# Expert biases as the weight of a constant last element, and scatters ahead of the reciprocal root, in an attention and mixture-of-experts kernel

## The chip, the cores and the metric

The kernel runs on one core of a Trainium2 chip. The metric is the device time of one execution in microseconds. Five engines work side by side: TensorE (PE in the profile, with its weight loads as PEld), VectorE (DVE), ScalarE (ACT), GpSimd (POOL) and SyncE (SP, which here only issues transfers). Sixteen DMA engines carry the transfers.

## What is computed

The reference takes x (64 sequences of 128 tokens, 256 features) and a context (64 x 128 x 192) and does, in float32:

```python
x = x + cross_attention(layernorm(x), ctx)      # 16 heads of 64, per sequence; Wproj, bproj
x = x + ffn(layernorm(x))
# ffn: probs = softmax(tokens @ gate_w.T)        # 8 experts
#      top2_w, top2_idx = top_k(probs, 2)
#      expert_out = silu(tokens @ expert_w[e].T + expert_b[e])
#      mixed = sum over the two chosen experts of top2_w * expert_out
#      out = mixed @ combine_w.T
```

The layernorm has no scale and no shift, so the 256 elements of a normalised row sum to zero (but for rounding).

## The kernel before

**Pairs and slots.** The 8192 tokens are 32 pairs of 256 tokens. The program of each engine is one loop over slots s, written `slots()`, with i = s // 8 the pair and u = s % 8 the position in it; slots -8 to -1 are the start. A slot handles two of the sixteen heads of pair i as a pipeline over several slots: queries and keys (`qk_ps`), scores (`s_ps`), the exponential on ACT (L828, into `probs`, which lies in `stage`), the sums on DVE (L1015), the division on POOL (`normalise_probs`, L1309), the transposes on PE (`pT_ps`, L607, the first PE work of a slot), attention times values (`o_ps`), its split into a high and a low part on POOL (`split_attended`, L1318 and L1320), and the projection (`proj_ps`). Float32 products are made of three matmuls of float32r parts: hi x hi, hi x lo, lo x hi; ACT makes the high parts and DVE or POOL the low ones.

**Norms.** DVE makes the statistics (bn_stats, bn_aggr), POOL the reciprocal root (`rsqrt`, L1299 to L1304: an add of eps and a pow), DVE the normalised rows (`normalise`, L992). For the second norm (n = 1) of pair i - 1 all three steps stand in slots u = 2 and u = 3 of pair i.

**Experts.** 28 pairs (SPARSE) go the sparse way. After the routing of a pair, POOL scatters its normalised rows `xn2` by expert into `sorted_x` with four indirect DMAs, one in each of the slots u = 0 to 3 two pairs later (`scatter`, L1322). When a chunk of pairs (8, 8, 6, 4, 2) is routed, DVE lists its blocks of 128 rows of one expert (`list_blocks`), 147 in all, and from then on one block a slot is loaded, transposed (`turn_block`), multiplied with the expert's weights (`expert`, L693), put through silu as tanh, and stored in `sorted_y`. POOL gathers the results (`gather`), ACT weighs them, PE transposes their sum and multiplies it by the combine weights (`combine`); such a pair of steps is a mix. The last 4 pairs go the dense way after attention is over: `dense` (L715) makes all experts' outputs for 256 tokens in 8 jobs a pair, each with a 512 wide result, and `dense_out` and `dense_add` on DVE collect them.

**Biases.** The expert biases are split into high and low parts and stored in a small table (`keep_bias`, L435). Each block loads its expert's two rows (`b_block`, L474), and a seventh matmul of ones with that tile adds them. Each dense job has a seventh matmul too, of `first_two` (ones in two rows) with `b_all` (L722 to L726).

**First loads and splits.** SP issues the loads of x, context and weights in the order of L497 to L508. The expert weights (256 x 2048) come in two halves of 128 rows, `WEIGHTS[6]` and `[7]`, over parts of `stage` that earlier weights held, so SP waits for DVE's splits first (L422). In slots 0 to 7 ACT makes the high part of one expert's weights (`weight_hi`, L804), POOL the low part (`weight_lo`, L1288), and SP stores both in `expert_table` (`keep_expert`, L428). Transfers issued by SP stand in one queue, the keys' spread `k_s<-qk_s` (L412) among them, without which no scores start.

Of the kernel before, what the change touches and what calls it, by code (L numbers as in the profile page):

```python
# [18 lines left out]
ROUND = 8388608.0  # L19

# [116 lines left out]
def xattn_moe_kernel(nc, x, ctxT, wq, wkv, wkv_rest, wproj, bproj, gateT, expertT, expert_b, combineT, out):  # L137
# [19 lines left out]
    bias_table = nc.dram_tensor("bias_table", [(REGIONS + 1) * 2, C], F32, kind="Internal").ap()  # L157

    with ExitStack() as stack:
# [15 lines left out]
        gate_raw = sb("gate_raw", [P, 2, E])  # L175
        pbias = sb("pbias", [P, C], F32R)
# [3 lines left out]
        first_two = sb("first_two", [P, P], F32R)  # L180
# [20 lines left out]

        bias_raw = xn2[1][0:E + 1, 0, :]
        bias_s = [xn2[0][0:E + 1, h, :].bitcast(F32R) for h in range(2)]
# [4 lines left out]
        b_block = [sb(f"b_block{r}", [P, C], F32R) for r in range(RING)]  # L208
        xbT = [hilo(f"xbT{b}", [P, 2, P]) for b in range(2)]
        mT_s = hilo("mT_s", [P, 2, N2])  # L210

# [30 lines left out]
        b_all = wkvr_s[0]  # L242
# [57 lines left out]
        bias_stored = sem("bias_stored")  # L300
# [8 lines left out]
        b_block_in = [sem(f"b_block_in{r}") for r in range(RING)]  # L309
# [33 lines left out]
        two_zero = sem("two_zero")  # L343
# [13 lines left out]
        def blocks_in_ring(r, n):  # L357
# [11 lines left out]
            (expertT[P:2 * P, :], stage[:, 1, :]),  # L369
# [22 lines left out]
        def _(sp):  # L392
# [42 lines left out]
            def keep_bias():  # L435
                sp.wait_ge(ebias_lo, 1)
                of_expert = bias_table.rearrange("(e h) c -> e h c", h=2)
                for h in range(2):
                    of = bias_s[h].bitcast(F32)
                    sp.dma_start(of_expert[0:E, h, :], of[0:E, :]).then_inc(bias_stored, 16)  # L440
                    sp.dma_start(of_expert[E:E + 1, h, :], of[0:1, :]).then_inc(bias_stored, 16)
                    sp.dma_start(of_expert[E + 1:E + 2, h, :], of[E:E + 1, :]).then_inc(bias_stored, 16)
                sp.wait_ge(bias_stored, 96)
                sp.wait_ge(zeroed, 2)
                sp.dma_start(pbias[0:2, :].bitcast(F32), bias_table[2 * (E + 1):2 * (E + 2), :]).then_inc(bias_in, 16)
# [14 lines left out]
            def load_expert(c, b, n):  # L460
# [7 lines left out]
                if n == 0:  # L468
                    sp.wait_ge(bias_stored, 96)
# [4 lines left out]
                sp.dma_start(b_block[r][0:2, :].bitcast(F32),  # L474
                             bias_table[bass.ds(e * 2, 2), :]).then_inc(b_block_in[r], 16)
# [17 lines left out]
            def load_biases():  # L493
                sp.dma_start(b_all[0:2, :].bitcast(F32).rearrange("h (e c) -> h e c", e=E),
                             bias_table[0:2 * E, :].rearrange("(e h) c -> h e c", h=2)).then_inc(dense_in[0], 16)

# [66 lines left out]
        def _(pe):  # L563
# [56 lines left out]
            def project(j, p):  # L620
# [5 lines left out]
                if j == 0 and p == HEAD_PAIRS - 1:  # L626
                    pe.wait_ge(bias_in, 16)
                    pe.wait_ge(const_r, 3)
# [40 lines left out]
            def gate(j, bank):  # L669
                pe.wait_ge(drained["turn_x1"], j + 1)  # L670
                if j == 0:
                    pe.wait_ge(gate_w_ready, 2)
# [5 lines left out]
            def rank(j, bank):  # L678
                pe.wait_ge(hot_done, j + 1)
                if j == 0:  # L680
                    pe.wait_ge(const_r, 3)
# [11 lines left out]
            def expert(n, bank):  # L693
                pe.wait_ge(drained["turn_block"], n + 1)
                pe.wait_ge(w_block_in[n % RING], 16 * (n // RING + 1))
                pe.wait_ge(b_block_in[n % RING], 16 * (n // RING + 1))
# [4 lines left out]
                terms.append((ones_s[:, :], b_block[n % RING][:, :]))  # L701
# [13 lines left out]
            def dense(n):  # L715
                m, q, t = SPARSE + n // DENSE_JOBS, n % DENSE_JOBS // 2, n % 2
                if n == 0:
                    pe.wait_ge(dense_in[0], 80)
# [711 lines left out]
```

## Time and profile before

| | us |
|---|---|
| median of 3 runs (lowest, highest) | 1630.62 (1629.04, 1634.59) |
| the profiled execution, its own time | 1637.44 |
| its span, first to last instruction | 1635.4 |
| busy in it: PE, DVE, ACT, POOL | 1537.0, 1264.0, 1062.0, 879.9 |

The durations below are of the profiled execution, whose time is 0.4% above the median of the others. A matmul's printed duration runs from its start to a modelled end and overlaps the next one; starts of neighbours show the pace. In the timeline view a row is: start, duration, engine, line, operation, out<-in, shape, and in brackets the idle time before it with what ended it.

### The profile page before, as it was taken

How to read it: one execution, taken by the hardware profiler on the slowest of the kernel's cores; microseconds unless marked ns; L12 is line 12 of the kernel's file. 1: busy time of each engine (PE TensorE's matmuls, PEld its weight loads, DVE VectorE, ACT ScalarE, POOL GpSimd, SP SyncE). 2: the span in 40 equal slices, each digit the busy share in tenths (PEclk: the TensorE clock that was granted, in tenths of full speed). 3: DMA queues.
4: the chain of work that ended last, by engine and by line, in shares of the span. 5: the costliest groups of instructions: out<-in, count | busy, mean ns of one | idle time of the engine just before them, and what ended most of it. 6: DMA issues, size and time to landing. Idle time of an engine off the chain costs nothing.

```text
span 1635.4 us, 39352 instructions
## 1 busy us (share of the span) xinstructions
PE 1537.0 (94%) x11891; PEld 1470.2 (90%) x11891; DVE 1264.0 (77%) x3135; ACT 1062.0 (65%) x2890; POOL 879.9 (54%) x1185
## 2 busy tenths in 40 slices
PE   4999999998999999999999999999999999999787
PEld 4899999998999999998999999899998998999675
DVE  5788888777888888877877888877778787776566
ACT  4766666665666766675767667666766666666433
POOL 4655555555545555576655545575656465644410
PEclk9999999999999999999999999999999999999999
DMA  6633333333577777344677667467777776877722
GB/s 226 203 85 91 92 91 92 91 91 95 173 216 223 223 217 210 101 123 128 201 224 227 204 213 217 135 188 226 230 227 211 220 229 198 248 218 216 273 64 78
DMA packets 179131, 286.99 MB, mean 175 GB/s; under 512 B 23575, under 2 KB 113900, under 8 KB 178668
## 3 DMA queue, kind: packets, MB, share of 16 engines
q1 hardware_dynamic: 168172, 255.11, 52.7%
q0 software_dynamic: 10752, 29.37, 5.8%
q8 instruction: 99, 1.62, 0.4%
q14 instruction: 108, 0.88, 0.2%
HBM read 155.66 MB, written 61.62 MB: 133 GB/s over the span
## 4 chain that ended last, share of the span: by engine, by line
PE 73%; DVE 10%; issue 6%; ACT 5%; POOL 4%; DMA 1%; SPq 0%; ACTq 0%; DVEq 0%; POOLq 0%
PE gen_ps L566 21%; PE qk_ps L566 15%; PE o_ps L566 9%; PE proj_ps L566 9%; PE s_ps L566 8%; PE pT_ps L607 6%; ACT stage L801 2%; PE gen_ps L690 1%; PE gen_ps L657 1%; PE gen_ps L665 1%; DMA k_s<-qk_s 1%; DVE sums L1015 1%; ACT v_s_hi L801 1%; POOL sorted_x L1328 1%; POOL stage L1309 1%
## 5 line engine op out<-in xcount | busy, mean ns | idle before, releaser
L828 ACT ACTIVATE stage<-s_ps,neg_max 128x128 f32<-128x128 f32 x1024 | 292.8, 371 | 105.8 <-DVE neg_max L1008 95.7
L1318 POOL CAST o_s_hi<-stage 128x256 fp32r<-128x256 f32 x256 | 102.2, 399 | 477.0 <-ACT stage L801 471.8
L1309 POOL TENSOR_TENSOR stage<-stage,inv_sums 128x512 f32<-128x512 f32 x256 | 266.8, 1042 | 15.9 <-DVE inv_sums L1017 15.9
L801 ACT CAST pT_s_hi<-pT_ps 128x512 fp32r<-128x512 f32 x256 | 150.9, 589 | 150.9 <-PE pT_ps L607 141.8
L566 PE MATMUL s_ps<-k_s,qk_s 128*128 128x256 f32 x1536 | 226.6, 283 | 4.1 <-DMA k_s<-qk_s 3.2
L1015 DVE TENSOR_REDUCE sums<-stage 128x4 f32<-128x512 f32 x256 | 172.9, 676 | 66.5 <-ACT stage L828 56.7
L960 DVE TENSOR_TENSOR pT_s_lo<-pT_ps,pT_s_hi 128x512 fp32r<-128x512 f32 x256 | 172.8, 675 | 56.0 <-ACT pT_s_hi L801 50.3
L960 DVE TENSOR_TENSOR qk_s<-qk_ps,qk_s 128x512 fp32r<-128x512 f32 x256 | 175.8, 687 | 41.8 <-ACT qk_s L801 39.0
L566 PEld LDWEIGHTS s_ps<-k_s,qk_s 128*128 128x128 f32 x1536 | 201.4, 191 | 4.9 <-DMA k_s<-qk_s 3.9
L1320 POOL TENSOR_TENSOR o_s_lo<-stage,o_s_hi 128x256 fp32r<-128x256 f32 x256 | 188.0, 734 | 21.1
L801 ACT CAST v_s_hi<-gen_ps 128x512 fp32r<-128x512 f32 x129 | 75.7, 587 | 177.2 <-PE gen_ps L566 173.3
L801 ACT COPY stage<-o_ps 64x256 f32<-64x256 f32 x512 | 188.4, 368 | 3.1
L566 PE MATMUL qk_ps<-xT_hi,wq_s_hi 128*128 128x256 f32 x512 | 166.7, 326 | 11.4 <-DVE wkvr_s_lo L971 6.5
L566 PE MATMUL o_ps<-pT_s_hi,v_s_hi 128*128 128x256 f32 x512 | 156.0, 305 | 22.4 <-DVE pT_s_lo L960 19.2
L1008 DVE TENSOR_REDUCE neg_max<-s_ps 128x4 f32<-128x512 f32 x256 | 174.4, 681 | 2.5 <-PE s_ps L566 2.5
L801 ACT CAST qk_s<-qk_ps 128x512 fp32r<-128x512 f32 x256 | 152.8, 597 | 24.8 <-PE qk_ps L566 18.2
L566 PE MATMUL proj_ps<-wproj_s_hi,o_s_hi 128*128 128x256 f32 x512 | 149.5, 292 | 12.5 <-POOL o_s_lo L1320 12.5
L607 PE MATMUL pT_ps<-ident,stage 128*128 128x128 f32 x1024 | 156.9, 276 | 2.2 <-POOL stage L1309 1.0
L566 PE MATMUL o_ps<-pT_s_lo,v_s_hi 128*128 128x256 f32 x512 | 145.2, 284 | 0.0
L566 PE MATMUL o_ps<-pT_s_hi,v_s_lo 128*128 128x256 f32 x512 | 145.2, 284 | 0.0
L566 PE MATMUL qk_ps<-xT_lo,wq_s_hi 128*128 128x256 f32 x512 | 144.5, 282 | 0.0
L566 PE MATMUL proj_ps<-wproj_s_hi,o_s_lo 128*128 128x256 f32 x512 | 143.9, 281 | 0.0
(358 smaller groups left out, 4706.1 us busy)
## 6 DMA issues: line engine op xcount, KB each, us to landing
w_block<-expert_table SPq DMA_DIRECT2D x147, 512.0 KB
k_s<-qk_s SPq DMA_DIRECT2D x512, 128.0 KB
stage<-sorted_x SPq DMA_DIRECT2D x147, 128.0 KB
sorted_y<-stage SPq DMA_DIRECT2D x147, 128.0 KB
x_raw<-in_x SPq DMA_DIRECT2D x32, 256.0 KB
c_raw<-in_ctxT SPq DMA_DIRECT2D x32, 256.0 KB, 3.3
stage<-in_x SPq DMA_DIRECT2D x32, 256.0 KB
x_kept<-x SPq DMA_DIRECT2D x32, 256.0 KB
```

The costliest lines, as they stand in the source:

```text
L566: mm = pe.matmul(out_ap, l, r, start=start and n == 0, stop=stop and n == len(terms) - 1, skip_group_check=skip)
L607: mm = pe.transpose(pT_ps[:, k * P:(k + 1) * P], probs[p % 2][:, k, :], ident[:, :])
L657: mm = pe.matmul(bank[:, a * N2 + t * P:a * N2 + (t + 1) * P], src[:, 2 * t + k, a * P:(a + 1) * P], ident[:, :], is_transpose=True, start ...
L665: mm = pe.transpose(bank[:, a * N2 + t * P:a * N2 + (t + 1) * P], src[:, t, a * P:(a + 1) * P], ident[:, :])
L801: last = act.copy(to, of)
L828: last = act.activation(probs[p % 2][:, k, :], s_ps[:, k * P:(k + 1) * P], ACT.Exp, bias=neg_max[p % 2][:, k:k + 1])
L960: last = dve.tensor_tensor(lo, of, hi.bitcast(F32), ALU.subtract)
L1008: dve.tensor_reduce(neg_max[p % 2][:, :], s_ps[:, :].rearrange("p (k n) -> p k n", k=4), AX_X, ALU.max, negate=True).then_inc(max_done, 1)
L1015: dve.tensor_reduce(sums[p % 2][:, :], probs[p % 2][:, :, :], AX_X, ALU.add).then_inc(sums_done, 1)
L1309: pool.tensor_tensor(probs[b][:, :, :], probs[b][:, :, :], inv_sums[b][:, :].unsqueeze(2).broadcast_to([P, 4, P]), ALU.mult).then_inc(prob ...
L1318: pool.tensor_copy(hi[:, :, :], o_full).then_inc(o_hi, 1)
L1320: pool.tensor_tensor(lo[:, :, :], o_full, hi[:, :, :].bitcast(F32), ALU.subtract).then_inc(o_lo, 1)
```

## The change

The last element of each row of the second norm is not computed: it is 1.0 always (set once in both `xn2` buffers; `normalise` writes 255 elements). Since a normalised row sums to zero, the product with a weight matrix is the sum over the other 255 elements with the last element's weights subtracted from theirs. So the last weight row becomes free to hold the bias. DVE subtracts the last row, which SP loads into all partitions for each expert (`load_last`), from the expert's weights (`expert_minus_last`); the second half of the expert weights is loaded without its last row, whose place takes `expert_b`. The same is done for the gate weights, with no bias (there the last row becomes zero). The bias matmuls of blocks and of dense jobs, their loads and their table go. `bproj` keeps its way, with its two parts now copied straight to `pbias`. On POOL, the four scatters of a pair stand ahead of `rsqrt` in their slot.

```diff
             (expertT[0:P, :], stage[:, 0, :]),
-            (expertT[P:2 * P, :], stage[:, 1, :]),
+            (expertT[P:2 * P - 1, :], stage[0:P - 1, 1, :]),
...
             def keep_bias():
                 sp.wait_ge(ebias_lo, 1)
-                of_expert = bias_table.rearrange("(e h) c -> e h c", h=2)
+                sp.wait_ge(zeroed, 2)
                 for h in range(2):
-                    of = bias_s[h].bitcast(F32)
-                    sp.dma_start(of_expert[0:E, h, :], of[0:E, :]).then_inc(bias_stored, 16)
...
+                    sp.dma_start(pbias[h:h + 1, :].bitcast(F32), bias_s[h].bitcast(F32)).then_inc(bias_in, 16)
+
+            def load_last(e):
+
+                wait(sp, minus_last, 2 * (e - RING + 1))
+                sp.dma_start(last_row[:, e % RING, :], expertT[2 * P - 1:2 * P, e * C:(e + 1) * C].broadcast_to([P, C])).then_inc(
+                    last_in[e % RING], 16)
...
                 sp.dma_start(w_block[r][:, :, :].bitcast(F32).rearrange("p a n -> p (a n)"),
                              expert_table[bass.ds(e * P, P), :]).then_inc(w_block_in[r], 16)
-                sp.dma_start(b_block[r][0:2, :].bitcast(F32),
-                             bias_table[bass.ds(e * 2, 2), :]).then_inc(b_block_in[r], 16)
...
-            sp.dma_start(bias_raw[0:E, :], expert_b.rearrange("(e c) -> e c", c=C)).then_inc(ebias_in, 16)
-            sp.dma_start(bias_raw[E:E + 1, :], bproj.rearrange("(e c) -> e c", c=C)).then_inc(ebias_in, 16)
+            sp.dma_start(gate_last[:, :], gateT[C - 1:C, :].broadcast_to([P, E])).then_inc(gate_in, 16)
+            sp.dma_start(bias_raw, bproj.rearrange("(e c) -> e c", c=C)).then_inc(ebias_in, 16)
             for n in range(5, 9):
                 load_weights(n)
+                if n == 7:
+                    sp.dma_start(stage[P - 1:P, 1, :], expert_b.rearrange("(o n) -> o n", o=1)).then_inc(w_in[7], 16)
+                    for e in range(RING):
+                        load_last(e)
...
+                if 0 <= s < E - RING:
+                    load_last(s + RING)
...
                 if s == SLOTS * pairs - 3:
                     load_experts(0)
-                    load_biases()
...
                 for a in range(2):
                     terms += three(xs, (w[:, a, :], w[:, 2 + a, :]), lambda y: y[:, a, :], lambda part: part)
-                terms.append((ones_s[:, :], b_block[n % RING][:, :]))
                 return products(bank[:, 0:C], terms)
...
                     terms += three(xT1[m], (w_all[0][a], w_all[1][a]), lambda y: y[:, a, rows], lambda w: w[:, cols])
-                terms.append((first_two[:, :], b_all[:, cols]))
                 products(dense_ps[n % DENSE_BANKS][:, :], terms).then_inc(made["dense"], 1)
...
                 elif n < COMBINE_SPLIT:
-                    act.wait_ge(w_in[6], 16)
-                    act.wait_ge(w_in[7], 16)
                     e = n - EXPERTS_FROM
+                    act.wait_ge(minus_last, 2 * (e + 1))
...
+            def expert_minus_last(e):
+                if e == 0:
+                    dve.wait_ge(w_in[6], 16)
+                    dve.wait_ge(w_in[7], 32)
+                dve.wait_ge(last_in[e % RING], 16 * (e // RING + 1))
+                last = last_row[:, e % RING, :]
+                for a, rows in enumerate((slice(0, P), slice(0, P - 1))):
+                    weights = stage[rows, a, e * C:(e + 1) * C]
+                    dve.tensor_tensor(weights, weights, last[rows, :], ALU.subtract).then_inc(minus_last, 1)
...
-                    normalise(i - 1, 1, x1, xn2[(i - 1) % 2], xn2_done)
+                    normalise(i - 1, 1, x1, xn2[(i - 1) % 2], xn2_done, C - 1)
...
+                if i == 0 and u == 0:
+                    dve.wait_ge(gate_in, 32)
+                    dve.tensor_tensor(gate_raw[:, :, :], gate_raw[:, :, :],
+                                      gate_last[:, :].unsqueeze(1).broadcast_to([P, 2, E]),
+                                      ALU.subtract).then_inc(gate_w_ready, 1)
+                if -1 <= s < E - 1:
+                    expert_minus_last(s + 1)
...
-            for r in range(RING):
-                pool.memset(b_block[r][:, :].bitcast(F32), 0.0)
...
+            pool.memset(ones_column[0], 1.0)
+            pool.memset(ones_column[1], 1.0).then_inc(const_c, 1)
...
                 if now:
                     normalise_probs(i, u)
+                if u < 4 and exists(i - 2) and i - 2 < SPARSE:
+                    scatter(i - 2, u)
                 if s in (-SLOTS + 1, 1):
                     rsqrt(i + 1, 0)
                 if u == 6 and i >= 0 and exists(i + 2):
                     rsqrt(i + 2, 0)
                 if u == 2 and before:
                     rsqrt(i - 1, 1)
-                if u < 4 and exists(i - 2) and i - 2 < SPARSE:
-                    scatter(i - 2, u)
```

## Rows read from the trace of the kernel before

**Rows 1.** The page, part 1: busy us, share of the span, instructions.

```profile
PE 1537.0 (94%) x11891; PEld 1470.2 (90%) x11891; DVE 1264.0 (77%) x3135; ACT 1062.0 (65%) x2890; POOL 879.9 (54%) x1185
```

**Rows 2.** Who waited for whom: us in total, times, longest us.

```profile
PE proj_ps L566 <- POOL o_s_lo L1320: 12.5, 17, 1.0
```

**Rows 3.** Busy time by stretch: us, busy (x), PEclk, DMA share, GB/s.

```profile
440.00:640.00 200.00, 199.98 (x1623) 195.49 (x1622) 162.85 (x412) 137.93 (x391) 102.39 (x141) 1.00 0.71 215
```

**Rows 4.** Timeline and groups by form of PE: the bias matmul of a block.

```profile
904.85 0.28 PE L566 MATMUL gen_ps<-b_block,ones_s 128*128 128x256 f32 x1
904.97 0.27 PE L607 MATMUL pT_ps<-ident,stage 128*128 128x128 f32 x1
...
L566 PE MATMUL gen_ps<-b_block,ones_s 128*128 128x256 f32 x147 | 41.9, 285 | 0.0
```

**Rows 5.** Timeline of PE: the bias matmul of a dense job and the next.

```profile
1528.06 0.40 PE L566 MATMUL qk_ps<-wkvr_s_hi,first_two 128*128 128x512 f32 x1
1528.29 0.40 PE L566 MATMUL s_ps<-wq_s_hi,x1T_hi 128*128 128x512 f32 x1
```

**Rows 6.** Busy time by stretch: the dense jobs after attention.

```profile
1575.00:1615.00 40.00, 37.85 (x195) 31.50 (x194) 35.39 (x82) 18.17 (x39) 8.07 (x8) 1.00 0.23 70
```

**Rows 7.** Timeline of POOL around u = 2 and 3: pair 1, then pair 2.

```profile
86.89 0.40 POOL L1318 CAST o_s_hi<-stage 128x256 fp32r<-128x256 f32 x1
...
125.33 0.20 POOL L1302 TENSOR_TENSOR var_eps<-mv,eps 128x2 f32<-128x2 f32 x1 [1.97 <-DVE mv L984]
...
126.52 1.08 POOL L1328 DMA_INDIRECT sorted_x<-xn,row_of  x1 [0.19 <-issue]
127.61 0.41 POOL L1318 CAST o_s_hi<-stage 128x256 fp32r<-128x256 f32 x1
...
130.05 1.03 POOL L1328 DMA_INDIRECT sorted_x<-xn,row_of  x1 [0.16 <-issue]
```

**Rows 8.** Timeline of PE: slot u = 3 of pair 1, then of pair 2.

```profile
84.81 0.27 PE L607 MATMUL pT_ps<-ident,stage 128*128 128x128 f32 x1
...
89.16 0.33 PE L607 MATMUL pT_ps<-ident,stage 128*128 128x128 f32 x1
...
124.17 0.27 PE L607 MATMUL pT_ps<-ident,stage 128*128 128x128 f32 x1
...
128.89 0.38 PE L566 MATMUL proj_ps<-wproj_s_hi,o_s_hi 128*128 128x256 f32 x1 [0.95 <-POOL o_s_lo L1320]
...
129.94 0.33 PE L607 MATMUL pT_ps<-ident,stage 128*128 128x128 f32 x1
```

**Rows 9.** Timeline of PE: slot u = 3 of pair 29, then of pair 30.

```profile
1387.88 0.27 PE L607 MATMUL pT_ps<-ident,stage 128*128 128x128 f32 x1
...
1394.82 0.27 PE L607 MATMUL pT_ps<-ident,stage 128*128 128x128 f32 x1
...
1440.97 0.27 PE L607 MATMUL pT_ps<-ident,stage 128*128 128x128 f32 x1
...
1447.73 0.27 PE L607 MATMUL pT_ps<-ident,stage 128*128 128x128 f32 x1
```

**Rows 10.** The page, part 5: a DVE tensor_tensor; then the stretch of pair 0.

```profile
L960 DVE TENSOR_TENSOR qk_s<-qk_ps,qk_s 128x512 fp32r<-128x512 f32 x256 | 175.8, 687 | 41.8 <-ACT qk_s L801 39.0
...
41.00:82.00 41.00, 39.30 (x301) 36.74 (x300) 30.40 (x59) 31.29 (x83) 28.55 (x36) 1.00 0.60 203
```

**Rows 11.** DMA issues up to 60 us, stretches, and PE's first scores.

```profile
stage<-in_expertT SPq DMA_DIRECT2D x2, 1024.0 KB, 6.6
...
xn<-in_expert_b SPq DMA_DIRECT2D x1, 8.0 KB
...
18.20:24.00 5.80, 5.76 (x30) 4.62 (x28) 2.58 (x4) 3.23 (x5) 0.73 (x1) 1.00 0.89 299
20.50:22.00 1.50, 1.46 (x9) 0.97 (x8) 0.71 (x2) 0.73 (x4) 0.00 (x0) 1.00 1.00 399
...
28.79 0.98 PE L566 MATMUL s_ps<-k_s,qk_s 128*128 128x256 f32 x6 [1.82 <-DMA k_s<-qk_s]
```

More of the change, by code:

```diff
@@ L175, in xattn_moe_kernel @@
         gate_raw = sb("gate_raw", [P, 2, E])
+        gate_last = sb("gate_last", [P, E])
         pbias = sb("pbias", [P, C], F32R)
@@ L200, in xattn_moe_kernel @@
         xn2 = [sb(f"xn2_{b}", [P, 2, C]) for b in range(2)]
-        bias_raw = xn2[1][0:E + 1, 0, :]
-        bias_s = [xn2[0][0:E + 1, h, :].bitcast(F32R) for h in range(2)]
+        ones_column = [y[:, :, C - 1:C] for y in xn2]
         x1T = hilo("x1T", [P, 2, N2])
@@ L207, in xattn_moe_kernel @@
         w_block = [sb(f"w_block{r}", [P, 4, C], F32R) for r in range(RING)]
-        b_block = [sb(f"b_block{r}", [P, C], F32R) for r in range(RING)]
         xbT = [hilo(f"xbT{b}", [P, 2, P]) for b in range(2)]
         mT_s = hilo("mT_s", [P, 2, N2])
+        bias_raw = x1[0:1, 1, :]
+        bias_s = [y[0:1, :, :].rearrange("p a n -> p (a n)") for y in xbT[0]]
+        last_row = sb("last_row", [P, RING, C])
         stage = sb("stage", [P, 4, 2 * D])
@@ L299, in xattn_moe_kernel @@
         table_stored = [sem(f"table_stored{r}") for r in range(RING)]
-        bias_stored = sem("bias_stored")
+        last_in = [sem(f"last_in{r}") for r in range(RING)]
+        minus_last = sem("minus_last")
         x1_saved = sem("x1_saved")
@@ L308, in xattn_moe_kernel @@
         w_block_in = [sem(f"w_block_in{r}") for r in range(RING)]
-        b_block_in = [sem(f"b_block_in{r}") for r in range(RING)]
         y_stored = [sem(f"y_stored{r}") for r in range(RING)]
@@ L626, in project @@
                 if j == 0 and p == HEAD_PAIRS - 1:
-                    pe.wait_ge(bias_in, 16)
-                    pe.wait_ge(const_r, 3)
+                    pe.wait_ge(bias_in, 32)
+                    pe.wait_ge(const_r, 2)
                 for t in range(2):
@@ L671, in gate @@
                 if j == 0:
-                    pe.wait_ge(gate_w_ready, 2)
+                    pe.wait_ge(gate_w_ready, 3)
                 for t in range(2):
@@ L680, in rank @@
                 if j == 0:
-                    pe.wait_ge(const_r, 3)
+                    pe.wait_ge(const_r, 2)
                 pe.matmul(bank[:, 0:2 * E], before_s[:, :], hot[:, 0:2, :].rearrange("p t e -> p (t e)"),
@@ L717, in dense @@
                 if n == 0:
-                    pe.wait_ge(dense_in[0], 80)
-                    pe.wait_ge(const_r, 3)
+                    pe.wait_ge(dense_in[0], 64)
                 if n == DENSE_JOBS // 2:
@@ L950, in _ @@
                     weight_hi(EXPERTS_FROM + u)
+                if i == 0 and u == 1:
+                    act.wait_ge(gate_w_ready, 1)
+                    act.copy(wgate[:, :, 0:E], gate_raw[:, :, :]).then_inc(gate_w_ready, 1)
                 if i == 1 and u == 0:
@@ L990, in x_stats, with normalise @@
                 norm_merge(0)
-            def normalise(j, n, src, to, done):
+            def normalise(j, n, src, to, done, width=C):
                 dve.wait_ge(rstd_done[n], j + 1)
                 for t in range(2):
-                    last = dve.tensor_scalar(to[:, t, :], src[:, t, :], mv[n][:, t, 0:1], rstd[n][:, t:t + 1],
+                    last = dve.tensor_scalar(to[:, t, 0:width], src[:, t, 0:width], mv[n][:, t, 0:1], rstd[n][:, t:t + 1],
                                              ALU.subtract, ALU.mult)
@@ L1044, in add_residual @@
                 wait(dve, xn2_done, j)
+                if j == 0:
+                    dve.wait_ge(ebias_lo, 1)
                 flat_x1, flat_xb = (y.rearrange("p t c -> p (t c)") for y in (x1[:, :, :], xb))
@@ L1266, in _ @@
                     if i - 1 < 2:
[L1267 to L1268 removed]
+                        dve.wait_ge(const_c, 3)
+                    normalise(i - 1, 1, x1, xn2[(i - 1) % 2], xn2_done, C - 1)
                 if u == 4 and nxt:
```

25 lines of the change are left out of this document (2 added, 23 removed).

## The prediction, made before the changed kernel was run

> **What bounds the kernel now.** I read the page first, then the waits, then the stretches, then the order of single instructions. The page shows TensorE (PE) busy for 94% of the span, far ahead of the others [rows 1]. The waits of PE say why it is not more: in the whole run it waits 12.5 us for POOL's `o_s_lo`, seventeen times [rows 2]. In the stretch from 440 to 640 us PE is busy for 199.98 of 200 us while VectorE (DVE) has 162.85 and ScalarE 137.93 [rows 3]. So in the slots that carry expert blocks each instruction taken from PE should shorten the slot. In the slots without blocks POOL has a say, and at the two ends DMA and DVE do. I therefore cost the change stretch by stretch against the profiled execution (span 1635.4 us, its own time 1637.44), and carry the difference to the median of the runs shown, 1630.62. A measurement of this kernel can tell about 0.3% (4.9 us) from no change.
>
> **The bias matmul of each block (removed).** A matmul's printed duration overlaps its neighbours', so the price is the distance between starts: the bias matmul starts at 904.85 and what follows at 904.97, so 0.12 us; there are 147 of them [rows 4]. All but 4 run before the last attention slot: 143 x 0.12 = 17.2 us. I keep all of it, since no other engine is near full there [rows 3]; the four in the tail I count at 0.3 in all. The bias row's own load (0.29 us on SP each) hid beside the expert's weights and is worth nothing.
>
> **The bias matmul of each dense job (removed).** Starts 1528.06 and 1528.29: 0.23 us [rows 5], four pairs by eight jobs, 32 x 0.23 = 7.4 us of PE. But from 1575 to 1615 us DVE is busy 35.39 of 40 us and PE 37.85 [rows 6]; with some 20 of the 32 jobs there (4.6 us) PE falls to about 33 and DVE is the next to be late. Of the 4.6 us I take 3, and 2 of the 2.8 of the other twelve jobs, where DVE waits for PE more often than PE for DVE: 5.0 us, bounds 2.5 and 7.4.
>
> **The scatter ahead of the reciprocal root (moved).** Three things stand in POOL's queue at slot u = 2: the root's two instructions, which cannot start before DVE has merged the statistics, the third scatter of the pair two before, and then the `o_s` split of u = 3. With scatters (second pair shown) the root begins at 125.33 after 1.97 us of idling, the scatter at 126.52 takes 1.08, and the split starts only at 127.61 with no idle time; without scatters (pair 1) the split follows the root at once, at 86.89 [rows 7]. PE then waits 0.95 us at the projection, and what comes next, POOL's softmax scaling, is late as well: from one group of `pT_ps` transposes to the next it takes 129.94 - 124.17 = 5.77 us, against 89.16 - 84.81 = 4.35 in pair 1 [rows 8]. After the move the scatter fits into the 1.97 us of idling (0.19 + 1.08). Price: 1.42 us a pair in the 10 pairs whose slot u = 3 has neither block nor mix (14.2). In 2 pairs with a mix but no block the wait of 0.95 is there but the combine hides the late scaling: with the overlapped end of the matmul 1.1 each (2.2). In the 16 pairs with blocks the wait shows no idle time, but the same slot takes 1394.82 - 1387.88 = 6.94 us with a scatter and 1447.73 - 1440.97 = 6.76 in pair 30, which has none [rows 9]: 0.18 x 16 = 2.9. Together 19.3 us; bounds 11.4 (twelve times 0.95 alone) and 19.3. Scatter 3, in u = 3, stays where it is.
>
> **The subtraction on DVE (added).** Sixteen tensor_tensor of 128 x 256 at the ends of slots -1 to 6, and one of 16 columns. A 128 x 512 one takes 687 ns [rows 10], so between 0.34 and 0.69 each, 5.5 to 11 us in all; I take 0.34. DVE is busy 30.40 of 41 us there [rows 10]: most fits the idle time before it takes the softmax sums, while in the three slots where it also does the statistics or the normalising nothing is free. Queued behind it are the sums and `pT_s_lo`, for which PE waits. I count 1.2 us, bounds 0 and 6. ScalarE, which now waits for `minus_last` ahead of the expert's split, has it one slot early. The normalise over 255 instead of 256 elements: nothing, bounds -0.1 and 0.1 a pair if an odd width cost a third of it. The shorter list of memsets on POOL hides behind the load of Wq.
>
> **The first loads (changed).** This is the term that decides. SP issues the two halves of the expert weights, and they land 6.6 us (median) later; the keys' spread is issued behind them on the same queue, and the first scores start at 28.79 when it lands, on the chain that sets the end [rows 11]. The new second half has 127 rows. The profile prints landings for loads of 128 rows and none for the load of 8 rows, `xn<-in_expert_b` [rows 11], which hints that a small count of rows is not handled like a full one (weakly: some transfers that repeat lack a landing too); 127 rows make no equal shares for 16 engines, only 1 or 127. I take it that the whole transfer goes to one DMA engine. What one engine moves: in the fastest stretch, 20.50 to 22.00, all 16 together move 399 GB/s at a share of 1.00, so 25 GB/s each; from 18.20 to 24.00 it is 299 GB/s at 0.89, so 21 [rows 11]. 127 x 8 KB = 1.04 MB take 41.7 or 49.5 us on one. I take 41.7, the nearer case, since the other engines will be idle. Its usual share of the load would have been 2.6 us, so it is 39.1 us late, the three broadcast rows (24 KB for each engine) add 1.0, and since that engine's queue was not full up to 28.79 about 1.6 comes back: 38.5 us. The keys' shares for that engine stand behind it in order, so the scores start near 67 us, PE having nothing else to do, and I add 0.5 for matmuls at half speed after that pause.
>
> The Trainium skill, page DMA: Bandwidth & Descriptors, section Why a DMA increments its semaphore by 16 and not by 1, says that the number of engines is the largest one up to 16 that divides the slowest dimension of both sides, and names 127 partitions as a case of one engine. By it the start is late by 38.5 us; by an even deal it would be about 1. No run so far shows a transfer of 127 rows.
>
> **The sum.** Less: 17.2 + 0.3 + 5.0 + 19.3 = 41.8 us. More: 38.5 + 0.5 + 1.2 = 40.2 us. Net -1.6, so the span comes to 1633.8, the profiled time to 1635.8 and the median to 1629.0: no change that can be told.
>
> **Rivals.**
> 1. The 127 rows are dealt out to all engines. Then the start costs only the broadcast rows and DVE, 1.0 + 1.2 + 0.5 us, and the time is 1630.62 - 41.8 + 2.7 = 1591.5. For it: the rows only show that small counts differ. Against: the divisibility. 0.17.
> 2. Slower: the single engine runs at the 21 GB/s of 18.20 to 24.00 [rows 11], since it also reads 8 KB rows from one place. Place: the wait of the first scores; price 7.8 us more, 1636.8. It makes the kernel slower by over 0.3% once the load takes 6.5 us more than I took, at under 21.6 GB/s. 0.13.
> 3. The scatter gives only the visible waits (11.4 instead of 19.3), because scatter 3 at the end of u = 3, 0.16 + 1.03 us at 130.05 [rows 7], then delays the next split, which it doesn't where the slot is long: 1636.9. For it: pair 1, my measure, has no scatter at all. Against: the 1.97 us of idling at u = 2 [rows 7] shows POOL with room in a slot of that length. 0.08.
>
> **How the numbers follow.** Forecast 0.62, rivals 0.17, 0.13 and 0.08. The forecast's own spread is about 5 us to each side, from the tail and the single engine's rate. The range 1615 to 1641 holds the forecast, rivals 2 and 3 and the bounds of the tail; it leaves out rival 1 and little more. Faster: 0.17 and a fifth of the forecast, 0.30. Slower: most of rivals 2 and 3 and a small part of the forecast, 0.18. Same: 0.52.
>
> **What would show it.** Right: a pause of PE from about 27 to 67 us ended by the landing of `k_s`, DMA busy a sixteenth in that time; 4.35 us between the `pT_ps` groups of u = 3; no wait of PE for `o_s_lo`; block slots shorter by 0.12; the root on POOL with no scatter behind it. Wrong: first scores near 31 us (rival 1), near 75 (rival 2), or the projection still waiting (rival 3).

## The result and the profile after

The changed kernel takes 1643.09 us (median of 12 runs, 1639.7 to 1645.75) against 1631.98 (12 runs, 1627.04 to 1637.51) for the kernel before on the same chip: a ratio of 1.0067, 95% interval 1.0054 to 1.0080, or 10.9 us more. The prediction said 1629.0, range 1615 to 1641, with 0.52 for no change and 0.18 for slower. Two of the twelve executions of one kernel below (`b_no_dense_bias`) took 1707.02 and 2489.31 us, at granted clocks of 0.845 and 0.557, and are left out of its ratio.

The page of the changed kernel: part 1 (busy us, share, instructions), the granted clock in 40 slices, and one group of part 5.

```profile
PE 1514.8 (92%) x11712; PEld 1453.6 (89%) x11712; DVE 1269.3 (77%) x3152; ACT 1060.3 (65%) x2890; POOL 877.2 (53%) x1182
...
PEclk8699999999999999999999999999999999999989
...
L564 PE MATMUL s_ps<-k_s,qk_s 128*128 128x256 f32 x1536 | 226.5, 283 | 39.1 <-DMA k_s<-qk_s 39.0
...
L564 PE MATMUL proj_ps<-wproj_s_hi,o_s_hi 128*128 128x256 f32 x512 | 146.9, 287 | 1.4 <-POOL o_s_lo L1333 1.4
```

TensorE has 22.2 us less work than before [rows 1], from 179 matmuls fewer, and still the kernel ends later. Two waits have changed places. The one for `o_s_lo` has gone from 12.5 us [rows 2] to 1.4. The one for the keys' copy `k_s`, 1.82 us for the first scores before [rows 11], is now 39.0, nearly all of it one wait at the start. Its place is in the next two views of the changed kernel: first the timeline (SP's issues with their lengths, PE's first scores), then busy time by stretch (us, busy of PE, PEld, DVE, ACT, POOL, PEclk, DMA share, GB/s).

```profile
18.58 16.64 SPq L500 DMA_DIRECT2D stage<-in_expert_b  x1
35.26 7.77 SPq L445 DMA_DIRECT2D last_row<-in_expertT  x3
...
53.85 7.88 SPq L413 DMA_DIRECT2D k_s<-qk_s  x6
66.22 1.65 PE L564 MATMUL s_ps<-k_s,qk_s 128*128 128x256 f32 x6 [38.59 <-DMA k_s<-qk_s]
```

```profile
22.00:26.00 4.00, 2.59 (x17) 2.01 (x15) 1.37 (x3) 3.64 (x5) 1.83 (x2) 1.00 0.06 27
30.00:34.00 4.00, 0.00 (x0) 0.00 (x0) 0.00 (x0) 0.00 (x0) 0.00 (x0) 0.50 0.06 27
```

From 22 to 34 us the sixteen DMA engines are busy for 0.06 of the time, one sixteenth, and move 27 GB/s: one engine carries the 127 rows of 8 KB (1.04 MB, 38.5 us at that rate). Between 18.20 and 24.00 the kernel before had a share of 0.89 and 299 GB/s [rows 11]. SP stands at the issue of an 8 KB transfer for 16.64 us. The clock is granted at 0.50 (1.2 of 2.4 GHz) in the pause.

The other half of the change shows in slot u = 3 of pair 2, on POOL and on PE.

```profile
162.76 0.19 POOL L1315 TENSOR_TENSOR var_eps<-mv,eps 128x2 f32<-128x2 f32 x1 [0.82 <-DVE mv L988]
163.03 0.72 POOL L1317 TENSOR_TENSOR rstd<-var_eps,minus_half 128x2 f32<-128x2 f32 x1
163.72 0.39 POOL L1331 CAST o_s_hi<-stage 128x256 fp32r<-128x256 f32 x1
```

```profile
161.60 0.60 PE L605 MATMUL pT_ps<-ident,stage 128*128 128x128 f32 x4
...
165.98 0.66 PE L605 MATMUL pT_ps<-ident,stage 128*128 128x128 f32 x4
...
492.12 0.60 PE L605 MATMUL pT_ps<-ident,stage 128*128 128x128 f32 x4
497.38 0.60 PE L605 MATMUL pT_ps<-ident,stage 128*128 128x128 f32 x4
```

The root now idles 0.82 us, not 1.97 [rows 7], and the split follows it with no scatter between them. The slot takes 165.98 - 161.60 = 4.38 us, where it took 5.77 [rows 8]: 1.39 of the predicted 1.42. The last two rows are slot u = 4 of pair 10, which has an expert block and no part in the move: 5.26 us, against 469.99 - 464.64 = 5.35 before. So the bias matmul's 0.12 [rows 4] comes out as 0.09 there.

In three stretches, bounded by the first and the last group of `pT_ps` transposes: the start is 38.1 us longer (71.88 against 33.78), the middle 33.2 shorter, and what follows the last group 0.6 longer (114.2 against 113.6). That makes the profiled spans differ by 5.5 us only, since the profiled execution of before (1637.44) was a long one: its middle took 1488.0 us, while in the traces of two kernels below whose middle is the same code (`b_127_rows`, `b_no_dense_bias`) it took 1482.7 and 1482.0. Against those, the middle of the changed kernel is 27.6 us shorter, where 35.3 had been predicted (17.2 + 19.3 - 1.2). And the tail, where 5.3 was predicted, gave nothing. The tail of one program also differs from trace to trace: it is 113.6 in the kernel before and 112.6 in `b_127_rows`, whose tail is the same code.

### The profile page after: what moved, and what is told of

Read it like the earlier page. It is cut to its first block, busy times and chain, and to the rows that moved or that the text cites. A ratio compares the mean times of both kernels' runs of the same rounds, so it can differ in the third digit from the quotient of the medians.

```text
span 1640.9 us, 38420 instructions
## 1 busy us (share of the span) xinstructions
PE 1514.8 (92%) x11712; PEld 1453.6 (89%) x11712; DVE 1269.3 (77%) x3152; ACT 1060.3 (65%) x2890; POOL 877.2 (53%) x1182
## 4 chain that ended last, share of the span: by engine, by line
PE 73%; DVE 12%; issue 6%; ACT 4%; SPq 3%; POOL 1%; DMA 1%; ACTq 0%; DVEq 0%; POOLq 0%
PE gen_ps L564 20%; PE qk_ps L564 16%; PE o_ps L564 10%; PE proj_ps L564 10%; PE s_ps L564 8%; PE pT_ps L605 6%; PE gen_ps L688 1%; PE gen_ps L655 1%; DVE sums L1019 1%; PE gen_ps L663 1%; DVE neg_max L1012 1%; ACT stage L795 1%; DVE pT_s_lo L954 1%; SPq L500 1%; DVE xn L999 1%
## 5 line engine op out<-in xcount | busy, mean ns | idle before, releaser
L564 PE MATMUL s_ps<-k_s,qk_s 128*128 128x256 f32 x1536 | 226.5, 283 | 39.1 <-DMA k_s<-qk_s 39.0
L564 PE MATMUL qk_ps<-xT_hi,wq_s_lo 128*128 128x256 f32 x512 | 145.4, 284 | 0.0
```

Of the source, the lines that this page charges most:

```text
L564: mm = pe.matmul(out_ap, l, r, start=start and n == 0, stop=stop and n == len(terms) - 1, skip_group_check=skip)
```

## The experiments

My theories after this: (1) the start is that one transfer on one DMA engine, and nothing else; (2) scatter and block bias gave about what was said; (3) the dense bias matmuls gave nothing, since VectorE is as late as TensorE there; (4) what the change adds costs more than I counted. The rivals stand in the expectations. Each ratio below is to the kernel before on the same chip; its distance from 1, multiplied by 1631 us, gives the difference stated. The intervals of the ratios are 2 to 4 us to each side.

**`a_split_load`: the 127 rows in two transfers.**

```diff
-            (expertT[P:2 * P - 1, :], stage[0:P - 1, 1, :]),
+            (expertT[P:P + 112, :], stage[0:112, 1, :]),
...
                 if n == 7:
+                    sp.dma_start(stage[112:P - 1, 1, :], expertT[P + 112:2 * P - 1, :]).then_inc(w_in[7], 16)
...
```

> The kernel after, with the 127-row load of the second expert half cut in two: rows 0 to 111 in one transfer and rows 112 to 126 in another; nothing else. Theory 1 (the 38.1 us by which the first transpose starts later is that one transfer on one DMA engine, and the issues blocked behind it): the first transpose of the probabilities starts 34 to 39 us earlier than in the kernel after, at about 34 to 37 us, and the time is about 1643 - 38 = 1605 us. Rival (the start is late because of the broadcast row loads, the extra transfers in SP's queue or the DVE subtractions): the start moves by under 10 us and the time stays above 1633 us.

1602.39 us, ratio 0.9827 (0.9814 to 0.9840): 28.2 us below the kernel before and some 39 below the changed one. The first transposes start at 38.55. The wait for the keys, in the waits of PE of this kernel from 20 to 45 us, is down from 38.6 us but not back to 1.8:

```profile
PE s_ps L565 <- DMA k_s<-qk_s: 4.8, 1, 4.8
```

**`b_127_rows`: that load alone, in the kernel before.**

```diff
-            (expertT[P:2 * P, :], stage[:, 1, :]),
+            (expertT[P:2 * P - 1, :], stage[0:P - 1, 1, :]),
...
+                if n == 7:
+                    sp.dma_start(stage[P - 1:P, 1, :], expertT[2 * P - 1:2 * P, :]).then_inc(w_in[7], 16)
...
```

> The kernel before, with the second expert half loaded as 127 rows in one transfer and the last row in another of its own; nothing else. Theory 1 (one engine carries 127 rows): 36 to 40 us slower, about 1670 us. Rival (the load alone is hidden, and only with the subtractions that wait for it does it cost): 0 to 10 us slower.

1667.32 us, ratio 1.0225 (1.0212 to 1.0238): 36.7 us slower, with no subtraction and no broadcast row in the kernel. The waits of PE from 20 to 75 us (total, times, longest us), then the busy times from 30 to 34:

```profile
PE s_ps L568 <- DMA k_s<-qk_s: 38.0, 1, 38.0
```

```profile
30.00:34.00 4.00, 0.00 (x0) 0.00 (x0) 0.00 (x0) 0.00 (x0) 0.00 (x0) 0.50 0.06 27
```

Shown from both sides, then: the count of rows makes the start.

**`a_two_engines`: 122 rows and 5 rows.** The diff is that of `a_split_load` with 122 in place of 112.

> The kernel after, with its 127-row load cut into 122 rows (2 x 61) and 5 rows. Theory (a transfer is dealt over the largest number of engines up to 16 that divides its rows: 122 rows go over 2): each of two engines moves 61 x 8 KB = 0.50 MB at the 27 GB/s that the window of one busy engine shows in the kernel after, 18.5 us in place of 38.5, so the first transpose starts some 18 to 20 us earlier, at about 53 us, and the time is about 1642 - 19 = 1623 us. Rival (any number of rows that is no multiple of 16 falls to one engine): as the kernel after, 1642 us. Second rival (122 rows spread over all engines, only 127 does not): as with 112 and 15 rows, 1602 us.

1620.77 us, ratio 0.9939 (0.9924 to 0.9953). The wait of PE for the keys (20 to 60 us):

```profile
PE s_ps L565 <- DMA k_s<-qk_s: 18.7, 1, 18.7
```

Half of 38.0: 61 rows an engine in place of 127. SP is held for less long here and other loads overlap this one, so the share in the pause is mostly above two sixteenths. From 44 to 46 us, at the end of PE's wait, it is 0.13, two sixteenths:

```profile
44.00:46.00 2.00, 0.00 (x0) 0.00 (x0) 0.00 (x0) 0.00 (x0) 0.00 (x0) 0.50 0.13 49
```

Both rivals fall. The rule of the Trainium skill, page DMA: Bandwidth & Descriptors, section Why a DMA increments its semaphore by 16 and not by 1, is that a transfer goes to as many engines as the largest number up to 16 that divides the rows. All three kernels agree with it: 127 rows on one engine (share 0.06), 122 on two (0.13), and 112 with 15 without a long wait (4.8 us).

**`b_scatter_first`: the move alone.**

```diff
+                if u < 4 and exists(i - 2) and i - 2 < SPARSE:
+                    scatter(i - 2, u)
                 if s in (-SLOTS + 1, 1):
                     rsqrt(i + 1, 0)
...
-                if u < 4 and exists(i - 2) and i - 2 < SPARSE:
-                    scatter(i - 2, u)
```

> The kernel before with the scatters issued ahead of the reciprocal roots on POOL; nothing else. The prediction's term: 10 pairs by 1.42, 2 by 1.1 and 16 by 0.18 = 19.3 us faster, about 1612.7 us. Rival of the prediction: only 11.4 us faster. What the traces of before and after show slot by slot (1.39, 1.2 and 0.18) makes 18.2 us.

1612.89 us, ratio 0.9888 (0.9874 to 0.9903): 18.3 us faster. Between its `pT_ps` groups slot u = 3 of pair 2 takes 4.38 us (5.77 before), of pair 16 5.73 (6.95), of pair 19 6.75 (6.95). The prediction's three sizes hold (1.42, 1.1 and 0.18), and its rival of 11.4 us falls.

**`b_no_block_bias`: only the blocks' bias matmul.**

```diff
-                terms.append((ones_s[:, :], b_block[n % RING][:, :]))
```

> The kernel before without the bias matmul of the 147 expert blocks (their loads stay; the experts' biases of the sparse pairs are left out). The prediction's term: 143 x 0.12 = 17.2 us faster, about 1613.6 us. What the slots of the kernels before and after show (0.10 a block beside the scatter's part): 14 to 15 us, about 1616 us. Rival (the slots with blocks are set by VectorE, so that the matmul was hidden): under 5 us faster.

1616.9 us, ratio 0.9906 (0.9889 to 0.9924): 15.3 us faster, 0.10 a block. In pair 11 seven of the eight slots, all with a block, lose 0.06 to 0.12 us each, but slot u = 3 only 0.03 (5.53 to 5.50). With the scatter moved first (from `b_scatter_first` to `b_three_gains`, below) the same slot loses 0.12 (5.35 to 5.23): before, the scatter on POOL had hidden the matmul there.

**`b_no_dense_bias`: only the dense jobs' bias matmul** and the load of its biases.

```diff
-                terms.append((first_two[:, :], b_all[:, cols]))
...
-                    load_biases()
...
```

> The kernel before without the bias matmul in its dense jobs and without the load of those biases (the experts' biases of the pairs computed densely are left out); nothing else. The prediction's term: 5.0 us faster (2.5 to 7.4), since TensorE is the bound there. Rival (the tail behind the last pair is set by VectorE, whose two operations for a job take 0.69 + 1.00 us against TensorE's 1.64 with the bias and 1.41 without): 0 to 1 us faster.

1629.77 us (median of all twelve), ratio 0.9990 (0.9979 to 1.0002): 1.6 us, not told from none. The stretch from 1580 to 1600, first of the kernel before, then of this one:

```profile
1580.00:1600.00 20.00, 19.64 (x100) 16.26 (x99) 17.00 (x45) 7.51 (x16) 8.07 (x8) 1.00 0.29 84
```

```profile
1580.00:1600.00 20.00, 18.75 (x94) 15.24 (x92) 19.14 (x43) 8.96 (x18) 1.13 (x2) 1.00 0.19 63
```

PE was busy for 19.64 of 20 us and DVE for 17.00; without the bias matmul it is DVE with 19.14, and PE has gaps. The trace of before has one reason. Two of the groups of DVE there, by source line (count: ns min/median/max, first and last start, forms):

```profile
L1108 DVE SCALAR_TENSOR_TENSOR x_raw<-stage,qk_ps x8: 677/689/689, 1529.1 to 1609.8; 128x512 f32<-128x512 f32 x8
...
L1131 DVE SCALAR_TENSOR_TENSOR xn<-x_raw,dense_w,xn x14: 479/485/543, 1531.7 to 1583.8; 128x256 f32<-128x256 f32 x14
```

Line 1108 runs 32 times (22.0 us), line 1131 56 times (27.1) and a first product 8 times (2.8): 51.9 / 32 = 1.62 us of DVE for a job. On PE two neighbouring jobs of before start so:

```profile
1602.53 0.39 PE L566 MATMUL pT_ps<-wq_s_hi,v_s_hi 128*128 128x512 f32 x1
1604.13 0.39 PE L566 MATMUL o_ps<-wq_s_hi,v_s_hi 128*128 128x512 f32 x1
```

That is 1.60 us for seven matmuls (the 1.64 of my expectations was a little high). Without the bias it is 1.37 for six. So DVE is level with PE before, and clearly the later one as soon as the bias is gone.

There is a second reason, behind the last dense job. From the end of that job's first DVE operation (line 1108) to the end of the program it takes 19.6 us before and 23.1 us in this kernel. The mixes are left there, each a chain through PE, ACT and DVE. Two of their starts on PE with the transposes between them, in the kernel before:

```profile
1615.36 0.36 PE L566 MATMUL gen_ps<-wcomb_s_hi,mT_s_hi 128*128 128x256 f32 x1 [2.16 <-DVE mT_s_lo L960]
...
1616.86 1.03 PE L657 MATMUL gen_ps<-ident,stage 128*128 128x128 f32 x8
...
1619.44 0.36 PE L566 MATMUL gen_ps<-wcomb_s_hi,mT_s_hi 128*128 128x256 f32 x1 [1.55 <-DVE mT_s_lo L960]
```

The same in this kernel, and its busy times in that stretch:

```profile
1603.81 0.55 PE L565 MATMUL gen_ps<-wcomb_s_hi,mT_s_hi 128*128 128x256 f32 x1 [3.69 <-DVE mT_s_lo L958]
...
1606.51 1.91 PE L656 MATMUL gen_ps<-ident,stage 128*128 128x128 f32 x8
...
1609.97 0.55 PE L565 MATMUL gen_ps<-wcomb_s_hi,mT_s_hi 128*128 128x256 f32 x1 [1.55 <-DVE mT_s_lo L958]
```

```profile
1603.00:1613.00 10.00, 7.64 (x34) 7.30 (x35) 3.71 (x8) 0.59 (x1) 0.00 (x0) 0.50 0.17 52
```

PE has run ahead of DVE, pauses 3.69 us instead of 2.16, and comes back at a granted clock of 0.50, where before has 1.00. The step to the next mix takes 6.16 us in place of 4.08, and the one after it 5.14 in place of 3.64: 3.6 us lost on the chain to the end, in these two traces. Every kernel here without the dense bias matmuls and with DVE's full work takes 21.1 to 25.0 us behind the last job. Of the four with these matmuls and full DVE work three take 19.5 or 19.6, but `b_scatter_first` takes 24.0 at the same half clock. So the half clock is shown to cost this much; that taking the matmuls away always brings it on is not.

**`b_light_vector` and `b_light_no_bias`: the same with less work on DVE.**

```diff
+                        to, y = to[:, 0:P // 2], y[:, 0:P // 2]
                         ins = dve.scalar_tensor_tensor(out=to, in0=y, scalar=w, in1=to, op0=ALU.mult, op1=ALU.add)
```

> The kernel before, whose weighted sums of the dense jobs (the second of VectorE's two operations for a job, 56 instructions of 0.48 us) run over 64 of 256 columns (the dense pairs' other columns are left unsummed). Partner of the next kernel. If TensorE with its 1.64 us a job is as late as VectorE with 1.62 us, taking time from VectorE alone gains little: 0 to 4 us, about 1629 us. If VectorE were the only bound of the tail it would gain some 10 us.

> The last kernel, and without the dense bias matmuls (the dense pairs' expert biases are left out too). Theory (VectorE's 1.62 us a job took the place of TensorE's 1.64 us as soon as the bias matmul was gone, which is why the dense term gave 1.0 us and not 5.0): with VectorE light the 22 matmuls behind the last attention pair give 0.23 us each, 4 to 5 us under the last kernel, about 1624.5 us. Rival (the tail is set by its gathers and mixed sums whatever the dense jobs cost): under 1.5 us below the last kernel.

1626.02 us (ratio 0.9958, 0.9943 to 0.9973) and 1616.88 (0.9903, 0.9886 to 0.9919). Light DVE alone gives 6.9 us, more than the 0 to 4 expected, so DVE was already late in places. With DVE light the same bias matmuls give 9.0 us (ratios 0.0055 apart, by their intervals some 3.6 us to each side), not 1.6; the expectation was 4 to 5, and all 32 matmuls hold no more than 7.4. In the profiled executions it takes from the last `pT_ps` group to the end 113.6 us before, 112.2 without the bias, 107.4 with light DVE, 101.9 with both: the matmuls give 1.4 and 5.5 us of the 7.4, since all 32 lie in that stretch (my expectation said 22). Two places explain most of the difference. Over the last sixteen dense jobs, whose bias matmuls make 3.7 us, the time goes from 31.6 to 32.4 us (four traces) down to 31.1 with full DVE work, and from 30.7 to 27.1, the whole 3.6, with light DVE. (Of the ten other kernels without the matmuls and with full DVE work, nine take 31.1 or 31.2, the changed one 33.7.) The first sixteen give no such clear figure: the end of the sixteenth varies by 3 us among the kernels without the matmuls. Behind the last job the kernel with light DVE and no bias takes 19.5 us again, with no half clock. So VectorE takes some 3 us of the term and the half clock behind it 3.5. In the stretch 1580 to 1600 of the last kernel PE is the full one again:

```profile
1580.00:1600.00 20.00, 20.00 (x105) 16.89 (x104) 17.47 (x46) 9.84 (x22) 2.84 (x3) 1.00 0.24 77
```

**`b_three_gains`: scatter first, no bias matmul of either kind,** nothing of what the change adds (its diff is the three above).

> The kernel before with the scatters ahead of the reciprocal roots, and without the bias matmuls of the blocks and of the dense jobs (the experts' biases are left out); nothing of what the change adds. Apart they gained 17.9, 14.1 and 1.0 us. If they add up: 33.0 us faster, about 1598 us, and what keeps the kernel with 112 and 15 rows at 1602.4 is the 4 to 5 us of work that the change adds at the start. Rival (the gains overlap, since VectorE or ScalarE becomes the bound of the same slots): 28 us faster, about 1603 us, and the added work costs nothing.

1599.12 us, ratio 0.9795 (0.9780 to 0.9810): 33.4 us faster; the parts alone gave 18.3 + 15.3 + 1.6 = 35.2. They add up within their intervals. Against it `a_split_load`, which has the same gains and the added work, is 5.2 us slower (0.9827), and 6.9 in its second set (0.9837, below). By the intervals each is good to 3 or 4 us. I had counted 2.2 for it (1.2 for the subtractions, 1.0 for the broadcast rows).

**`a_one_column`: the subtractions narrowed.**

```diff
-                    weights = stage[rows, a, e * C:(e + 1) * C]
-                    dve.tensor_tensor(weights, weights, last[rows, :], ALU.subtract).then_inc(minus_last, 1)
+                    weights = stage[rows, a, e * C:e * C + 1]
+                    dve.tensor_tensor(weights, weights, last[rows, 0:1], ALU.subtract).then_inc(minus_last, 1)
```

> The kernel with 112 and 15 rows, whose subtractions of the last row touch one column of each expert's 256 (the other columns keep the weights that they have, so the last element's share is not taken out of them). It prices the 16 subtractions of 0.37 us and more on VectorE. The prediction's term: 1.2 us (0 to 6), so about 1601 us. Rival (they delay each slot of pair 0, whose periods rose by 0.9 us at two places between the kernels before and after): 3 to 5 us, about 1598 us.

1603.8 us, ratio 0.9829 (0.9813 to 0.9846): no gain. In its trace pair 0 is 2.0 us shorter than with full subtractions (37.94 against 39.95), more than the 1.2 us of the whole term, but the medians don't show it.

**`a_keys_ahead`: the keys' first spread before the last loads.**

```diff
-            for n in range(5, 9):
+            for n in range(5, 7):
                 load_weights(n)
...
                 if u >= 6 and exists(i + 1):
                     spread_keys(i + 1, u - 6)
+                if s == -2:
+                    load_weights(7)
...
+                    for e in range(RING):
+                        load_last(e)
+                    load_weights(8)
...
```

> The kernel with 112 and 15 rows, and the loads of the second expert half, of the expert biases, of the first three broadcast rows and of combineT moved on SP behind the keys' first spread (and the loads of x and ctx of pair 1 ahead of it). Theory (in the kernel with 112 and 15 rows TensorE still waits 4.8 us for the first k_s, whose transfer stands behind these loads; before waited 1.8): the first transpose starts 4 to 7 us earlier than its 38.55 us, and the time is about 1602.4 - 5 = 1597 us. Rival (the wait only moves to the first subtraction, which needs the same loads): no gain, 1602 us.

1602.11 us, ratio 0.9830 (0.9812 to 0.9849). The wait for the keys falls to 2.3 us and the first transposes start at 34.18, 4.4 us earlier; the median doesn't move. The next three kernels ran together on one chip: the one with 112 and 15 rows once more, the one with the keys ahead once more, and the latter with narrow subtractions.

> The kernel with 112 and 15 rows once more, as the partner of the next two on one chip: 1602.4 us, ratio 0.983 to the kernel before.

> The kernel with 112 and 15 rows whose keys' first spread goes ahead of the expert loads, once more. If what is won at the start (4.4 us at the first transpose, of which pair 0 gives back 1.2 us) reaches the end: 3 us below its partner, about 1599.5 us. Rival (the later stalls, where TensorE idles and comes back at a lower granted clock, take it back): within 1 us of its partner.

> The last kernel with the subtractions on one column of each expert's 256 (the other columns keep the weights that they have). If the start and the subtractions are the whole price of what the change adds, it comes to the time of the kernel with the three gains alone, ratio 0.9795, about 1598 us, 4 to 5 us below the kernel with 112 and 15 rows. Rival (the price lies elsewhere, as in the 0.1 us that every attention pair lasts longer, 2 to 3 us in all): about 1600.5 us or more.

1604.07 us (0.9837, 0.9817 to 0.9857), 1601.87 (0.9828, 0.9806 to 0.9851) and 1602.41 (0.9828, 0.9808 to 0.9847). The second lies 2.2 us below the first, between the two expectations and inside the spread; narrow subtractions add nothing, so start and subtractions together are not the whole price. The start itself turns out to vary: in this trace the 112 and 15 rows had their first transposes at 35.37 us, where the first trace had 38.55. Comparing two starts from single traces, as I did for "4.4 us", was worth little.

**`a_one_engine_last`: the 127 rows in one transfer, but issued last.**

```diff
...
+            sp.wait_ge(w_lo_dve, OVER[7])
+            sp.dma_start(stage[P - 1:P, 1, :], expert_b.rearrange("(o n) -> o n", o=1)).then_inc(w_in[7], 16)
+            for e in range(RING):
+                load_last(e)
+            load_weights(8)
             load_ctx(1)
             load_x(1)
+            load_weights(7)
```

> The kernel after, with its 127-row load in one transfer as it is, but issued behind the expert biases, the first three broadcast rows, combineT, and ctx and x of pair 1, not ahead of them. In the kernel after SP sat 16.6 us on the issue behind the 127-row load and 39 us over the following ones, and the first k_s landed at 66.2 us. Theory (the last of the small transfers' descriptors wait in the same engine's queue, each issue in turn, so that the keys come 4 to 6 us after the 127 rows are through): keys at about 61 to 62 us, time about 1642 - 4.5 = 1637 us. Rival (only the one engine's 38.5 us count, wherever the others stand): within 1 us of the kernel after, 1642 us.

1641.96 us, ratio 1.0058 (1.0043 to 1.0072), against 1.0067 with the order of the change: my theory fell, the rival holds. SP no longer stands 16.64 us at the bias row; it stands 27.44 at the keys' spread instead, and the scores start no earlier than at 66.22:

```profile
21.82 27.44 SPq L413 DMA_DIRECT2D k_s<-qk_s  x6
...
66.79 1.65 PE L566 MATMUL s_ps<-k_s,qk_s 128*128 128x256 f32 x6 [39.46 <-DMA k_s<-qk_s]
```

The long issue is a symptom. What the two orders have in common is the 1.04 MB that one engine moves ahead of the keys.

## Why the prediction was wrong

Its parts against the runs, in us:

| part | predicted | measured alone |
|---|---|---|
| 127 rows on one engine | +38.0 | +36.7 |
| scatter ahead of the root | -19.3 | -18.3 |
| bias matmul of the blocks | -17.5 | -15.3 |
| bias matmul of the dense jobs | -5.0 | -1.6 |
| the three gains together | -41.8 | -33.4 |
| other added work | +2.2 | +5.2 to +6.9 |
| sum | -1.6 | +10.9 (the change itself; these rows add up to +8.5 to +10.2) |

The prediction's 38.5 for the load held 1.0 for the broadcast rows, and its 0.5 for matmuls at half speed stood apart. Here the 1.0 is with the added work, and the 0.5 with the load, where `b_127_rows` measures it.

The largest step, the deal of 127 rows, was right, by the divisibility and by its size: one sixteenth of the DMA engines busy, PE's pause ended by `k_s` at 66 us where 67 was said. The rate was 27 GB/s, not 25, and the term 1.3 us too high. At 27 GB/s the transfer takes 38.5 us; less the 2.6 of its usual share, and with the 0.5 for half speed, that is 36.4. So the error of the rate (3.2 us) was in part made good by the 1.6 that I let come back, which doesn't show. Rival 1 (dealt over all engines), rival 2 (21 GB/s) and rival 3 (scatter worth only 11.4) are all out. No rival had the cause of the miss.

Two steps failed, each in a term of its own. Together they are 6 to 8 us of the miss of 12.5.

**One is the price of the added work**, 2.2 us where 5.2 to 6.9 were measured: the step "I count 1.2 us, bounds 0 and 6" took the low value. It and the next are about as large. The traces place part of it. Pair 0 takes 37.6 us with the three gains alone and 39.9 in both traces of the 112 and 15 rows, 2.3 more; narrow subtractions take 2.0 of it back, so the subtractions cost at least 2.0 in that trace, where 1.2 was said. The first transposes start at 34.45 with the three gains and at 38.55 and 35.37 here, 4.1 and 0.9 later. In the pairs behind it nothing is left: pairs 2 to 7 take 0.1 us longer each, but pairs 1 to 30 together take 1370.2 and 1369.4 us against 1370.5. Yet neither the narrow subtractions nor the earlier keys brought the median down. The stretch behind the last transposes, 112.6 and 115.5 us in two traces of the one program, varies by as much as is looked for. What makes up the rest of this price stays open.

**The other, better explained, is "Of the 4.6 us I take 3, and 2 of the 2.8"**, the dense bias matmuls, 5.0 us where 1.6 were measured. I divided the gain between PE and DVE from their busy shares over 40 us [rows 6], and put DVE's 35.39 of 40 down as room. The two costs of one job, 1.60 us on PE and 1.62 on DVE, stood in the same trace; side by side they leave nothing where DVE is the later one. Over the last sixteen jobs 3.7 us of matmuls gave some 0.5, and 3.6 once DVE was light. And I had put PE's clock in the tail at nothing: PE ran ahead, paused, and did the next two mixes at half clock, which cost 3.5 us. The 7.4 us of the matmuls, less 3.2 for DVE and 3.5 for the clock, are 0.7, where 1.6 by the medians and 1.4 by the traces were measured.

Smaller: the block term was sized by the spacing of starts, 0.12, for all 143; by the medians it came to 0.10, and the eight slots of pair 11 lose 0.62 us together, least in slot u = 3, where POOL's scatter hid it. The scatter term fell 1.0 us short; its kernel has 4.4 us more behind the last dense job than before (24.0 against 19.6), at half clock. The three gains together came out 1.8 us less than apart, which is inside the spread, and pair 11 shows no such loss (0.19 and 0.62 us apart, 0.87 together). With that difference counted the list closes: 8.4 us of gains too many, 3.0 to 4.7 of price too few, less 1.3 for the load, make 10.1 to 11.8 of the 12.5 us between -1.6 and +10.9.

The range ended at 1641 and the result is 1643.09. With two sums of 40 us against each other, 5 us to each side was too narrow: I had given bounds for the terms and then not used the upper one for DVE (6 us) in the range.

The version to keep is `a_split_load`: all that the change does, with the 127 rows in two transfers, 1602.4 and 1604.1 us in two sets. It beats the kernel before by 1.6 to 1.7% and the changed one by 2.3 to 2.4%. With the keys ahead (1602.1 and 1601.9) it is no slower, and no gain is shown.

## What to carry to other kernels

Count the rows of every transfer: taking one row out of 128 moved a megabyte from sixteen DMA engines to one, cost 37 us, and undid gains of 33 us. Cut such a load so that each piece divides well. And before an instruction is costed as a gain in a loop that two engines share, put the cost of one iteration on each engine side by side; a busy share of 0.88 over the stretch does not mean that the second engine has room. Where the lightened engine then pauses, look at its granted clock behind the pause: here 3.5 us were lost again to it.

## What I had not expected of the hardware

- SP stood at an issue behind the load that one engine carried: 16.64 us for a transfer of 8 KB, 27.44 for six of the keys' spread. With the load cut in 112 and 15 rows the 8 KB issue takes 0.25 us. That the one engine's queue was full is my reading and not shown. Here a long issue pointed to a transfer ahead of it that used one engine.
- One DMA engine moved 27 GB/s for 12 us and more, in two kernels alike, above its share of the fastest stretch of all sixteen (399 / 16 = 25, [rows 11]).
- Two traces of one and the same program differ by 3.2 us at the first transposes (38.55 and 35.37).
- The middle of the same code took 1488.0 us in one trace and 1482 to 1483 in two others. Most of it lies in pair 0 (39.1 against 37.4 and 37.5) and in pairs 26 to 30 (266.2 against 263.7 and 263.8). In one slot there, pair 29's first, in which the blocks' list is made, the kernel before took 10.0 us, the two others 9.07 and 9.77, and the changed one 8.45; the granted clock around it was 0.83 before and 1.00 in the changed one (rows: before, then after):

```profile
1362.00:1372.00 10.00, 7.56 (x52) 7.32 (x52) 9.00 (x35) 5.61 (x17) 4.92 (x6) 0.83 0.53 161
```

```profile
1370.00:1380.00 10.00, 7.48 (x64) 7.25 (x64) 9.38 (x35) 6.22 (x20) 6.08 (x7) 1.00 0.53 178
```
